# Projection written in the layout of the residual streams, the chain between images one body ahead, input halos issued by GpSimd

## The reference, cut to what matters

```python
x = x + _L0_conv_ref(_gn(x), ...)   # 1x1 conv to q, k, v; attention in 4x4 windows, 16 heads of size 1; 1x1 projection + bias
x = x + _L1_conv_ref(_gn(x), ...)   # 3x3 conv, 16 -> 16
x = x + _L2_conv_ref(_gn(x), ...)   # a 4x4 grid of cells, each a 3x3 conv + bias + relu with outputs right, up, down
x = x + _L3_conv_ref(_gn(x), ...)   # 3x3 conv on input rounded to 8 bits, its scale the maximum over all images
```

## Time and profile before

| | |
|---|---|
| time, median of 3 runs | 3595.39 us (3593.41 to 3597.88) |
| profiled execution | 3595.5 us, its span 3593.3 us |
| PE busy | 2928.5 us, 81% of the span |
| DVE busy | 2176.1 us, 61% |
| ACT busy | 2130.6 us, 59% |
| POOL busy | 23.2 us, 1% |
| mean granted TensorE clock | 0.922 |
| HBM read, written | 16.40 MB, 12.85 MB |

### The profile page before, as it was taken

One profiled execution on the slowest core, in us unless ns is written; L12 is line 12 of the kernel. 1 busy time (PEld: TensorE's weight loads), 2 busy tenths in 40 slices (PEclk: granted clock), 3 DMA queues, 4 the chain that ended last, 5 costly groups with the idle time before them and its releaser, 6 DMA issues.

```text
span 3593.3 us, 87404 instructions
## 1 busy us (share of the span) xinstructions
PE 2928.5 (81%) x39244; PEld 1226.3 (34%) x39244; DVE 2176.1 (61%) x1878; ACT 2130.6 (59%) x2437; POOL 23.2 (1%) x67
## 2 busy tenths in 40 slices
PE   5683699789968898789968998789968997889953
PEld 5681233233323332233323332233323332333311
DVE  5655991479936794579836893679737892040003
ACT  1101976577737675577727774576737673767633
POOL 0000000000000000000000000000000000000000
PEclk9896899899979999899989999899989998999976
DMA  2002657466555745476545855575546664685566
GB/s 44 0 1 36 86 69 91 55 89 94 73 64 73 109 65 74 64 95 87 73 56 77 114 65 74 66 95 81 75 59 86 97 78 55 87 118 73 70 108 125
DMA packets 111065, 269.52 MB, mean 75 GB/s; under 512 B 95184, under 2 KB 96080, under 8 KB 98768
## 3 DMA queue, kind: packets, MB, share of 16 engines
q1 hardware_dynamic: 110672, 263.67, 54.3%
HBM read 16.40 MB, written 12.85 MB: 8 GB/s over the span
## 4 chain that ended last, share of the span: by engine, by line
PE 61%; ACT 11%; DVE 9%; SPq 8%; issue 7%; DMA 4%; POOLq 0%; DVEq 0%; POOL 0%; ACTq 0%
PE conv_banks L761 32%; PE conv_banks L774 17%; ACT pair L634 6%; PE conv_banks L794 4%; ACT half L634 3%; SPq L436 3%; DMA half<-half 2%; PE side_banks L699 2%; PE conv_banks L751 2%; SPq L449 2%; SPq L448 1%; DVE half L934 1%; DVE pair L934 1%; PE side_banks L726 1%; PE conv_banks L844 1%
## 5 line engine op out<-in xcount | busy, mean ns | idle before, releaser
L634 ACT ACTIVATE pair<-conv_banks,b_cells 32x784 f32<-32x784 f32 x1368 | 1282.8, 938 | 790.7 <-PE conv_banks L774 719.1
L761 PE MATMUL conv_banks<-pair,w_cells 128*32 128x392 f32 x17664 | 1567.1, 504 | 49.1 <-issue 26.6
L774 PE MATMUL conv_banks<-half,w_cells 64*32 64x392 f32 x18432 | 910.8, 525 | 202.3 <-ACT half L634 58.1
L761 PEld LDWEIGHTS conv_banks<-pair,w_cells 128*32 128x32 f32 x17664 | 538.7, 109 | 1024.9 <-issue 946.4
L634 ACT ACTIVATE half<-conv_banks,b_cells 32x392 f32<-32x392 f32 (+1 forms) x848 | 569.9, 672 | 175.4 <-PE conv_banks L774 132.1
L774 PEld LDWEIGHTS conv_banks<-half,w_cells 64*32 64x32 f32 x18432 | 345.0, 110 | 746.9 <-issue 715.5
L620 ACT ACTIVATE scores<-scores 128x1792 f32<-128x1792 f32 x106 | 180.2, 1700 | 104.0 <-DVE scores L959 102.4
L947 DVE TENSOR_TENSOR scores<-qkv 128x1792 f32<-128x1792 f32 x106 | 214.1, 2019 | 36.8 <-ACT qkv L615 36.4
L957 DVE TENSOR_REDUCE score_max<-scores 128x112 f32<-128x1792 f32 x106 | 214.1, 2020 | 13.1 <-DVE scores L949 2.8
L949 DVE TENSOR_TENSOR scores<-scores,rel_bias_sb 128x1792 f32<-128x1792 f32 x106 | 214.6, 2025 | 3.6
L959 DVE TENSOR_TENSOR scores<-scores,score_max 128x1792 f32<-128x1792 f32 x106 | 214.6, 2025 | 3.6
(11 more groups left out here) (85 smaller groups left out, 1206.3 us busy)
## 6 DMA issues: line engine op xcount, KB each, us to landing
pair<-pair SPq DMA_DIRECT2D x384, 391.9 KB, 8.6
half<-half SPq DMA_DIRECT2D x352, 192.4 KB, 5.5
x_block<-in_x SPq DMA_DIRECT2D x64, 98.0 KB, 4.6
stream<-x_block SPq DMA_DIRECT2D x128, 49.0 KB, 2.6
x_scratch<-stream SPq DMA_DIRECT2D x8, 784.0 KB, 10.0
pair<-x_scratch SPq DMA_DIRECT2D x8, 784.0 KB, 15.2
out_dram<-pair SPq DMA_DIRECT2D x32, 196.0 KB, 4.2
half<-half SPq DMA_DIRECT2D x176, 7.1 KB, 4.6
```

What stands on the lines that cost most here:

```text
L634: done = nc.scalar.activation(dst, src, ACT.Relu, bias=b_ap)
L761: done = nc.tensor.matmul(conv_ps[32 * q:32 * q + 32, n + b, 0:QN], w, P[row][:, QG * s:QG * (s + 1), QX * q + kx:QX * (q + 1) + kx], star ...
L774: done = nc.tensor.matmul(conv_ps[32 * q:32 * q + 32, n + h, 0:QN], w_all[rows, at:at + 32], T[rows, QG * u:QG * (u + 1), QX * q + kx:QX * ...
```

## The change

1. The projection's weights are arranged so that its output lands in the stream layout: four matmuls of 128 x 112 in place of one of 128 x 224. `XB` gets the stream layout and is loaded from HBM in it (`load_xb`, 8 DMAs, unit 4); `residual` adds in place. `fetch_x1` with its 16 DMAs is gone; `normalise_stream(1)` and `add_conv1` read XB.
2. XA is read by nothing after the seventh `normalise_chunk`, so `load_x` of the next image stands at unit 52 and waits for `xn_ready`.
3. `turn` replaces `to_stream`: it does norm 1 of image i, `normalise_stream(1)`, and statistics, norm 0 and first chunk of image i+1. `mean0`, `var0`, `qkv` 0, both halves of `conv1`, `mean2` and `var2` move from units 1 to 10 of the next body to units 59 to 66 of this one; `proj` and `qkv` stand 4 to 18 units earlier. The loop now runs bodies 0 to 4; body 5 has tables of its own.
4. The halo copies of the normalised streams (six DMAs, twice per image) are issued by GpSimd, in program order with its powers.
5. Cell (0,0) joins the shared cells; DVE empties one cell behind each of j=4 to 7. The statistics' PSUM columns are separate for each norm.

```diff
-INPUT = ("half", 2)
+INPUT = ("input", 2)
...
+PE_MID = {0: [("qkv", 1, 0)], 4: [("proj", 0, 0), ("qkv", 2, 0)], 10: [("proj", 1, 0), ("qkv", 3, 0)],
+          27: [("proj", 2, 0), ("qkv", 4, 0)], 43: [("proj", 3, 0), ("qkv", 5, 0)],
+          48: [("proj", 4, 0), ("qkv", 6, 0)], 52: [("proj", 5, 0)], 57: [("proj", 6, 0)], 58: [("mean1", 0, 0)],
+          59: [("var1", 0, 0), ("mean0", 0, 1)], 60: [("var0", 0, 1)], 62: [("qkv", 0, 1)],
+          63: [("conv1", 0, 1)], 64: [("conv1", 1, 1)], 65: [("mean2", 0, 1)], 66: [("var2", 0, 1)]}
...
+SP_MID = {4: ["xb"], 34: ["x3"], 52: ["xa"]}
...
+SHARED_MID, SHARED_LATE, SHARED_LAST = [(0, 0), (0, 1), (0, 2), (0, 3)], [(0, 0), (0, 1), (0, 2), (0, 3)], []
...
+            def load_xb(i):
                 if not (isinstance(i, int) and i == 0):
+                    sp.wait_ge(added1, i * NQ)
                 for q in range(NQ):
                     for r in range(2):
+                        at = 32 * q + 16 * r
+                        sp.dma_start(XB[at:at + 16], x[i].rearrange("c (q g r) w -> q r c g w", q=NQ, r=2)[q, r]
+                                     ).then_inc(xb_in, 16)
...
+            def send_input(i, which):
+                pool.wait_ge(c_ready, i * 2 * NQ + (which + 1) * NQ)
+                pool.sem_inc(pool_held, 1)
+                send_half(pool, INPUT)
...
+            with pool.Fori(0, B - 2) as b:
                 rstd_of(b, 2)
+                send_input(b, 1)
                 rstd_of(b + 1, 1)
+                send_input(b + 1, 0)
+                rstd_of(b + 2, 0)
...
+                    rhs = att[:, k % 3].rearrange("p (w g r j) -> p r g w j", g=2, r=2, j=PW)
+                    for h in range(2):
+                        dst = proj_ps.rearrange("p (g x) -> p g x", g=2)[:, :, XW * h:XW * (h + 1)]
+                        for r in range(2):
+                            done = nc.tensor.matmul(dst, wp_sb[:, h, r], rhs[:, r], start=r == 0, stop=r == 1)
+                    done.then_inc(proj_done, 1)
...
+            def turn(i, ch, last_read, more):
 
                 residual(i, WROWS - 1)
                 dve.wait_ge(x1_ready, (i + 1) * WROWS)
+                block_stats(1, XB[:].rearrange("p g w -> p (g w)"), st1, mv1, ch)
+                if more:
+                    dve.wait_ge(x_in, (i + 2) * N_LOAD * 16)
+                    block_stats(0, XA[:], st0, mv0, ch)
+                centre(i, 1, ch, mv1, dev1[:])
+                if more:
+                    centre(i + 1, 0, ch, mv0, nm0[:, 3:4])
+                spread(i, 1, ch, nm1)
+                normalise_stream(1, nm1, i, last_read)
+                if more:
+                    spread(i + 1, 0, ch, nm0)
+                    normalise_chunk(i + 1, 0)
...
                     if not early:
-                        if j == 3:
-                            empty(m, SHARED_MID[:2])
+                        if 4 <= j < 8:
+                            empty(m, SHARED_MID[j - 4:j - 3])
+                        if j == 6:
                             finish(m, m)
-                        if j == 4:
-                            empty(m, SHARED_MID[2:])
```

More of the change, by code:

```diff
@@ L129, in n_dmas @@
 def n_dmas(key):
-    return 6 if key[0] == "half" else 2
+    return 2 if key[0] == "pair" else 6
 def count_halos():
@@ L167, in halo_values @@
     return got
[L170 to L186, removed]
@@ L209, in vec_value, with sides @@
     return max(min(m, B - 2), 0) * per + (n_shared(B - 2, NB) if m == B - 1 else 0) + n_shared(m, k + 1)
-def sides(m, first, mid, late, last={}):
-    return {-1: first, B - 2: late, B - 1: last}.get(m, mid) if isinstance(m, int) else mid
+def sides(m, first, mid, before, late={}, last={}):
+    return {-1: first, B - 3: before, B - 2: late, B - 1: last}.get(m, mid) if isinstance(m, int) else mid
 W_PAIR, W_SINGLE, _n = {}, {}, 0
@@ L378, in conv_block, with wait_halos @@
         out_stored = sem("out_stored")
-        def wait_halos(eng, m, what, kinds=("pair", "half")):
+        def wait_halos(eng, m, what, kinds=("pair", "half", "input")):
             for key, value in halo_values(m, what):
@@ L502, in _ @@
             sp.dma_start(w_all[:], wc).then_inc(w_in, 16)
[L503 removed]
+            load_xb(0)
             load_x(1)
             sp.wait_ge(zeroed, N_ZERO)
[L506 removed]
+            body(-1)
             with sp.Fori(0, B - 3) as m:
[L508 to L511 removed]
+                body(m)
+            body(B - 3)
+            body(B - 2)
+            body(B - 1)
             sp.wait_ge(conv_done, NS)
@@ L650, in _ @@
             body(-1)
-            with act.Fori(0, B - 2) as m:
+            with act.Fori(0, B - 3) as m:
                 body(m)
+            body(B - 3)
             body(B - 2)
@@ L821, in _ @@
             side_step(-2, "var1", 0)
+            side_step(-1, "mean0", 0)
+            side_step(-1, "var0", 0)
             pe.wait_ge(zeroed, N_ZERO)
@@ L824, in _ @@
             body(-1)
-            with pe.Fori(0, B - 2) as m:
+            with pe.Fori(0, B - 3) as m:
                 body(m)
+            body(B - 3)
             body(B - 2)
@@ L1124, in body @@
                         residual(i, j // SUBS - 1)
-                to_stream(i, side)
-                side.end()
+                last_read = unit_base(m) + 1 + units_in(m).index(((1, 1), RIGHT, 1))
+                more = not (isinstance(m, int) and m == B - 3)
+                turn(i, side, last_read, more)
+                if more:
+                    side.end()
             dve.wait_ge(consts_in, N_CONST * 16)
@@ L1132, in _ @@
             body(-1)
-            with dve.Fori(0, B - 2) as m:
+            with dve.Fori(0, B - 3) as m:
                 body(m)
+            body(B - 3)
             body(B - 2)
```

203 lines of the change are left out of this document (109 added, 94 removed).

## The result

The changed kernel takes 3407.5 us (3405.5 to 3410.4), the one before 3594.4 us (3592.9 to 3597.9): a ratio of 0.9479, 95% interval [0.9463, 0.9496]. The forecast was 3363 with a range of 3240 to 3460, so the direction and the range held and the point was 44 us low. The profiled execution has a span of 3408.5 us against 3593.3.

A forecast was written before the change was run, and what follows sets the result against it. No engine was full; PE had most work (81%), losing 72 us a period to waits and low clock. Start -11, body -1 +17, bodies 0 to 5 -201, body 6 -38: -233, giving 3363 us, range 3240 to 3460.

The forecast's parts named there:

- Part 1, the projection: Each proj on PE takes 1.57 us instead of 0.57: +1.0 us, seven times a period, +7.
- I take the upper, since its row has this very shape: Choice of +1.0 us per proj from bounds +0 to +1.0, priced by sixteen 128 x 112 matmuls at 0.39 us each.
- a proj under 1 us: Sign of a wrong forecast at the projection, where about 1.6 us in 8 passes was expected.
- The chain a body earlier: PE's waits for statistics and conv1's halos go, 10.97 + 19.89 us plus low clock 2.8 + 1.6; first stretch 93 instead of 143.3.
- The gap at the loop's seam, which no edit touches: PE's gap at the loop's seam, releaser issue, stays at 2.73 + 1.41 us, 4.1 in the first stretch's sum.
- Part 4, GpSimd: At unit 62 qkv 0 waits behind GpSimd's six halo issues: stall 6d - 4.3, 2 us a period, from 0 to 14.
- d: Time GpSimd takes to issue one halo DMA; taken as 1 us, from 0.5 to 3.1.
- its halos are there unless d is above 1.5: conv1, a unit and a qkv later, doesn't wait for halos, taking 5.5 us from issue to landing.
- The rival of a slow GpSimd: GpSimd's issues take 3.1 us each, stall 14.3 instead of 2, seven times: +86, 3449 us; chance 0.13.
- the one of a queue that makes it slower than before: POOL's queue uses up the period's 33.5 us gain above 6.6 us per issue; 3655 us at 8; chance 0.04.
- Part 5, the middle: Units 14 to 42: DVE decides, PE waits 18.7 us in all, plus 5 for low clock; 107.6 us, before 106.1.
- (0,0) to +14: DVE's share of cell (0,0) lasts until 14 us after unit 14 starts, ahead of attention step j=5, to +29.7.
- The rival that nothing is late in the middle: DVE and PE interleave without waits at full clock, middle 89 us: -18.7 x 6, 3250 us; chance 0.22.

The follow-up runs named there:

- the window sums: Changed kernel with the first image's attention sums over windows reading 112 neighbouring columns instead of every 16th; 3366.6 us, one run.
- the combination: Changed kernel plus conv1 one unit later, first load at unit 35, (0,0) shared behind step 5, end-of-layer statistics behind step 7 and its residual; 3315.7 us, ratio 0.9219.

## Why the prediction was right, and where its terms were off

**Part 1, the projection: wrong in its size.** +1.0 us each was forecast from the earlier trace rows, +0.4 was measured, 4 us less per period, and a proj of 0.99 us is also what the forecast had named as a sign of being wrong ("a proj under 1 us"). The step that failed is "I take the upper, since its row has this very shape": the row has the shape, but not the layout of the operand that is read, as the window sums show. The estimate that was set aside, +0.3, worked out from the Trainium skill (TensorE: Matmul & The Clock Gate, LDWEIGHTS), was the nearer one. The trace doesn't bear out its price of a load, though: the projection's loads have 186 ns and more, not 107.

**The chain a body earlier: right.** The waits of 10.97 and 19.89 us and the low clock behind them went, as did 18.70 at the start and 23.08 in body 6. Unit 0 of the first body came at 333.79 us (forecast 334), body 6 to the end got 39.8 us shorter (forecast 38). The last stretch is 163.61 for 163.6; two errors of some 3 us cancel in it, the cheaper projections and conv1's wait.

**"The gap at the loop's seam, which no edit touches": wrong.** It costs 10.7 us with its low clock (7.86 + 1.3 + 1.5), and 4.1 were in the sum. The step took a gap with the releaser issue for a constant. The edit that touched it is the change's own part 4, by the way of the DMA engines and not by GpSimd's queue.

**Part 4, GpSimd.** A stall of 2 us at qkv 0 was forecast with d = 1. d is 0.48, which is the forecast's lower bound, and qkv 0 doesn't wait. The wait is at conv1, 3.5 to 4.0 us and 1.4 to 2.7 of low clock: "its halos are there unless d is above 1.5" failed, because it took SP's 5.5 us from issue to landing for GpSimd's copies. The large ones of this group have 9.5 to 10.4 and the two small ones, issued last, 13.3 to 13.8. The rival of a slow GpSimd named the right customer with the wrong mechanism; the one of a queue that makes it slower than before had no part in it.

**Part 5, the middle: right in its sum, in part in its mechanism.** Waits of 18.7 us were forecast in it, 19.8 are there (11.8 released by DVE, 8.0 by ACT), and the stretch is 5 us longer than forecast. That the sums of the waits are so near is partly luck: the forecast had 13.5 by DVE, some 3 for halos and none of this size by ACT, and waits released by ACT were among its signs of being wrong. At units 30 and 40 DVE is late by 4.5 and 4.9 us, where 3.6 and 6.5 were forecast. But "(0,0) to +14" as the first link of the lateness fell: without DVE's share of (0,0) the two waits are the same. What makes them is that a step of 15 us stands ahead of each share; moved, the first goes and the second shrinks. The rival that nothing is late in the middle is refuted at the changed kernel, but its remark that DVE idles ahead of unit 14 pointed to the edit that is worth 22 us.

**Body -1: missed.** The load at unit 40 was never costed there. SP issues the eight copies from 551.59 on, and the wait is 14.02 us; with the load five units earlier it is gone.

In sum, by the profiled executions: body -1 is 10 us longer than forecast and bodies 0 to 5 together 39, 370.7 instead of 364.2 each. Per looped period the terms are +6.6 (seam), +5 (middle), +3 to +5 (conv1) and -3.5 (projections outside the middle): 375 to 377 for 373.3 to 375.3 measured.

What stays open: for the first group, how much of the 10 us to its landing is what else is moved at that time. SP's queue has 46% and GpSimd's 29% of the engines' time between 1312 and 1333, and with SP as the issuer the large copies of this group took 8.0 to 8.2. For the second group the 5.3 us of the run with conv1 one unit later show that GpSimd's way adds nothing of note to SP's 5.2. No run took the other traffic away from the first group.

## What to carry to other kernels

A gap called issue at the end of a looped body can be a fetch of code, and it then queues with the kernel's own copies: look at what is issued in the microseconds before the branch, and move that copy, or the branch, before thinking of unrolling. Price an instruction from a row that has the same reading pattern, not only the same shape. When an engine serves the bottleneck engine in a fixed order, list what stands directly ahead of each late service; a service that is merely earlier in the list may be innocent.

## What the runs showed of the hardware

- PE's gap at a taken branch, read here as the fetch of its code, is 3.7 to 4.1 us where no halo packets were in front of it (four seams in each of four runs; in two of these runs the packets came in the gap, behind the branch) and 7.7 to 8.0 us behind 0.5 MB of halo packets.
- DVE's seam took 12.36 us while the first group of halos was on its way; its four seams come to 38 to 50 us in all runs in which GpSimd issued that group. About half of such a gap only covers a wait: in the combination DVE starts its scores 6.5 us after ACT's copy of qkv is done (1285.18, 1291.69), and with the loops written out it starts at once, behind a wait of 6.30 us for that copy. With SP as the issuer DVE also starts as soon as the copy is done, 8.92 us after its last instruction, so the seam was at most that long there. Why it is longer than PE's wasn't tested.
- GpSimd issues a 192 KB copy in 0.48 us. It lands after 8.8 us at the median of the changed kernel and SP's after 5.2, but GpSimd's second group after 5.3 where no pair copies were under way. With two 392 KB pair copies of SP in front it took 10.1.
- A matmul with 128 columns of weights and 112 of fp32 data, moving operand in steps of 64 bytes: 0.39 us (6.29 for sixteen); in runs of 16 bytes: 0.25 us (0.99 for four); in one run of 448 bytes: 0.23 us (3.74 for sixteen). The mean of a record, two of which make a matmul, is 375, 289 and 299 ns; records at the lower clock are in these means.
- Behind waits of 3.6 to 7.9 us the granted clock was at its lower level of 1.2 GHz for a while (0.50 from 1378.50 to 1386.00), and 48 matmuls that take 4.2 us took 5.6 to 6.9.
